# A hand-scheduled RWKV, FP4 FFN and attention kernel: the decay constant goes from VectorE's subtraction to the bias of ScalarE's Relu passes, and every engine's order of calls and waits is rewritten

## Chip, cores, metric

One core of a Trainium2 chip. The metric is device time in microseconds; all data are float32. Engines: PE (TensorE; PEld is its weight load), DVE (VectorE), ACT (ScalarE), POOL (GpSimd), and SP, which issues the transfers.

## What is computed

`x` is 16 sequences of 512 tokens with 128 channels. It passes through an initial layer norm, 4 RWKV layers, an FFN with blockwise FP4 rounding of inputs and weights, a causal attention, and the FFN again, each with a residual. The part that the arithmetic edit touches is the recurrence of an RWKV layer, per channel and over the tokens `t`, with `k`, `v` from the matrix products, `w = exp(time_decay)`, `u = time_first`:

```
a, b, m = 0, 0, -1e38                    # running numerator, denominator, maximum
for t: q = max(m, u + k)                 # the output of the token
       y = (exp(m-q)*a + exp(u+k-q)*v) / (exp(m-q)*b + exp(u+k-q))
       n = max(m - w, k)                 # the state for the next token
       a, b, m = exp(m-w-n)*a + exp(k-n)*v, exp(m-w-n)*b + exp(k-n), n
```

## The kernel before

A job `r` (0 to 63) is one sequence in one RWKV layer: layer `r // 16`, sequence `r % 16`, a tile of 128 partitions by 512. FFN jobs `n` run from 0 to 31 (first FFN, then second), attention jobs from 0 to 15. Each engine has one function with a loop `for t in range(FIRST, TICKS)`, here called ticks. The body of the loop is a list of calls written out by hand, each with a lag: `sub_d(t - 4)` handles job `t - 4` in tick `t`, and does nothing while that job is out of range. So the list and its lags are the engine's order of work; across engines only semaphores tie the ticks together. FFN jobs start at tick 69 (`FFN_AT`), attention at 85, the second FFN at 94, and there the lists mix calls of several parts.

The steps of an RWKV job that the prediction uses, with their lines in the profile:

- DVE: `bn1`, `bn2` (statistics, L230), `variances` (L320, L321), three mixes `mix_rt`, `mix_v`, `mix_t` (L334, L341, L327; from job 10 on; both tensors in SBUF), `scan_pp` (L350, running maximum), `sub_d` (L358), `mul_rv` (L366), `mul_s1` (L373), `scan_bb` (L380), `scan_aa` (L388), `gated` (L396), `rwkv` (L403), `add_xa` (L409), `mix_k`, `mix_r` (L421, L429), `gate` (L436). `init_affine` (L301, L303) runs for the first 16 jobs.
- ACT: `args` (L858, L859: two Relu passes over `dd`, one with scale -1), `seeds` (L882, L884), `exp_r` (L876), `exp_k` (L870), `keep_h1` (L843), `exp_d` (L865), `norm1`, `norm2` (L800), `tanh_r` (L850), `square_1` (L891), `relu` x4 (L912), `square` x2 (L919), `keep_past` (L904), `tanh_c` (L925).
- POOL: `add_xb` (L718), `add_den` (L690), `arg_r` (L684), `norm1_rest` (two chunks of 128, L658), `first_past` (L713, only for the first two jobs of a layer), `rsqrts` (the power, L650, and L652), `mul_y` (L701), `norm2_rest` (three chunks, L658), `sub_dh1` (L677), `scaled_p` (L707), `add_num` (L696).
- PE: `turn1`, `turn2` (L1089), `keys` (L1130), `ff_keys` x4 (L1192), `ff_values` x2 (L1210), `ff_gate` (L1199), `receptance`, `output`, `values` (L1155, L1178, L1143).

The chain through which a job's normalised tile reaches the recurrence is: `norm1_rest` on POOL and `norm1` on ACT, `turn1` on PE (waits for both), `keep_h1` on ACT, and behind it in ACT's order `exp_d`, for which `scan_bb` on DVE waits.

Before: `pp` is the running maximum after the decay; `sub_d` computes `dd = (k + w) - pp`, `args` takes `relu(dd)` and `relu(-dd)`, `arg_r` clips `dd` with `capt = CAP - u + w`, and `exp_r` takes `exp(... + now)` with `now = u - w`. `vecs_done` counts the 7 small vector steps at the start. `Waits.wait_ge` leaves out a wait that an earlier one on the same engine already covers.

Of the kernel before, what the change touches and what calls it, by code (L numbers as in the profile page):

```python
# [8 lines left out]
ALU = mybir.AluOpType  # L9
# [23 lines left out]
LN2_LAG = 6  # L33
# [3 lines left out]
FIRST = -2  # L37
# [39 lines left out]
def hybrid_program(nc, x_in, weights, vecs, rows, fp4w, qkv, wout, mask, ident, out):  # L77
    ctx = ExitStack()
    with ctx:
# [29 lines left out]
        capt, now = sb("capt", [128, L]), sb("now", [128, L])  # L109
# [61 lines left out]
        in_x, capt_done, ready = sem("in_x"), sem("capt"), sem("ready")  # L171
# [41 lines left out]
        VECS = 7  # L213
# [8 lines left out]
        def vector():  # L222
# [74 lines left out]
            def init_affine(b):  # L297
                if 0 <= b < NB:
                    w.wait_ge(small_here, 48)
                    w.wait_ge(n_in.z, b + 1)  # L300
# [9 lines left out]
            def variances(s):  # L310
                if 0 <= s < NR + LN2_LAG:
                    lo, hi = 0 if s < NR else NT, 2 * NT if s >= LN2_LAG else NT
                    rs, st = n_1.rs2[s % 3][:, :, lo:hi], n_1.st2[s % 3][:, lo:hi, :]
                    w.wait_ge(n_1.z, min(s - 2, NR))
# [4 lines left out]
                    w.wait_ge(n_2.stats, s - LN2_LAG + 1)  # L319
# [24 lines left out]
            def scan_pp(r):  # L344
                if 0 <= r < NR:
                    w.wait_ge(vecs_done, VECS)
                    w.wait_ge(consts, PADS)
                    w.wait_ge(d_done, r - 1)
                    w.wait_ge(k_done, r + 1)
# [41 lines left out]
            def gated(r):  # L391
                if 0 <= r < NR:
                    w.wait_ge(rwkv_done, r - 1)
                    w.wait_ge(sr_done, r + 1)
                    w.wait_ge(num_done, r + 1)
# [123 lines left out]
            def a_mask(n, i):  # L519
                if n in range(NB):  # L520
                    last = chunk(pS[i], i)
                    w.wait_ge(att_here, 48)
                    w.wait_ge(sim_mm, NT * n + i + 1)
                    e.tensor_tensor(last, last, msk[:, :], ALU.add).then_inc(msk_done, 1)

            def a_max(n, i):
                if n in range(NB):
                    w.wait_ge(a_x, n - 1)
                    w.wait_ge(msk_done, NT * n + i + 1)
# [8 lines left out]
            def a_add(n):  # L538
                if n in range(NB):
                    w.wait_ge(ari_done, n + 1)  # L540
                    w.wait_ge(a_bias, n + 1)
                    w.wait_ge(pv_mm, n + 1)
# [7 lines left out]
            for t in range(FIRST, TICKS):  # L550
                a_inverse(att_job(t - 5))
                rwkv(t - 6)
                sub_d(t - 4)
                mul_up(ffn_job(t - 4), 0)
                mul_up(ffn_job(t - 4), 1)
                bn2(t - 7)
                fx_sub(ffn_job(t - 2))
                fx_scale(ffn_job(t - 1))
                fh_add(ffn_job(t - 5), 0)
                mix_k(t - 8)  # L560
                mix_r(t - 8)
                mul_up(ffn_job(t - 4), 2)
                gated(t - 5)
                fh_sub(ffn_job(t - 5), 0)
                mul_up(ffn_job(t - 4), 3)
                variances(t - 1)
                fx_inverse(ffn_job(t - 1))
                mix_rt(t - 3)
                mix_v(t - 3)
                fh_max(ffn_job(t - 4))  # L570
                init_affine(t)
                mix_t(t - 3)
                a_mask(att_job(t - 4), 0)
                fh_scale(ffn_job(t - 4))
                a_max(att_job(t - 4), 0)
                fh_add(ffn_job(t - 5), 1)
                fh_inverse(ffn_job(t - 4))
                fh_sub(ffn_job(t - 5), 1)
# [862 lines left out]
```

## Time and profile before

| | us |
|---|---|
| median of 3 runs | 1366.13 |
| lowest, highest | 1358.09, 1373.18 |
| the profiled execution | 1361.77 |
| its span | 1360.5 |

The span runs from the first to the last instruction; 1.3 us lie around it. The granted TensorE clock has a mean of 0.994 of 2.4 GHz. Busy shares of the span: PE 94%, DVE 91%, ACT 90%, POOL 88%.

### The profile page before, as it was taken

The page shows a single profiled execution, that of the slowest core. Times are in us where ns is not written, and L with a number is a line of the kernel's source. Part 1 is how long each engine was busy: PE and PEld are TensorE (multiplying, and loading weights), DVE is VectorE, ACT ScalarE, POOL GpSimd, SP SyncE. Part 2 cuts the span into 40 slices and gives each one's busy share as a digit, 9 for nine tenths or more (in the row PEclk, how much of TensorE's full clock was granted, in tenths as well). Part 3 has the DMA queues.
Part 4 walks back from the last instruction along what each step waited for, and adds up shares of the span by engine and source line. Part 5 has one row for each costly group of instructions (what it writes and reads, how often), then busy time and mean ns, then how long its engine had stood idle before and what let it go on. Part 6 is the DMA issues. An engine that isn't in the chain of part 4 may idle for free.

```text
span 1360.5 us, 23452 instructions
## 1 busy us (share of the span) xinstructions
PE 1272.4 (94%) x7177; PEld 916.7 (67%) x7177; DVE 1243.0 (91%) x2235; ACT 1221.0 (90%) x2347; POOL 1198.7 (88%) x1401
## 2 busy tenths in 40 slices
PE   3789999999999999999999999989999998999997
PEld 1346666766677766767766666766777776678776
DVE  6998999999999999999999999679999477988995
ACT  4789999999999999999999999977787899999875
POOL 6898999999999999999999999989998456765884
PEclk9889999999999999999999999999999999999999
DMA  6020000000000000000000000010000000000011
GB/s 180 0 76 1 1 17 1 1 1 1 1 1 1 2 1 1 1 1 1 1 1 1 1 2 16 25 32 24 16 2 0 1 1 1 1 16 17 25 32 40
DMA packets 26925, 18.55 MB, mean 14 GB/s; under 512 B 1072, under 2 KB 26160, under 8 KB 26800
## 3 DMA queue, kind: packets, MB, share of 16 engines
q1 hardware_dynamic: 26800, 17.05, 4.2%
q8 instruction: 58, 0.95, 0.3%
q14 instruction: 67, 0.55, 0.1%
HBM read 12.85 MB, written 4.19 MB: 13 GB/s over the span
## 4 chain that ended last, share of the span: by engine, by line
PE 42%; POOL 32%; DVE 10%; issue 10%; ACT 5%; DMA 0%; POOLq 0%; SPq 0%; DVEq 0%; ACTq 0%
PE ps L1210 9%; POOL z L658 7%; PE ps L1192 7%; POOL ln_rs L650 4%; PE ps L1089 3%; POOL rv L696 3%; PE ps L1269 3%; PE ps L1319 2%; PE ps L1241 2%; POOL er L690 2%; POOL p L707 2%; PE ps L1248 2%; PE ps L1178 2%; PE ps L1155 2%; POOL W L747 2%
## 5 line engine op out<-in xcount | busy, mean ns | idle before, releaser
L1210 PEld LDWEIGHTS ps<-W,kf 128*128 128x128 f32 x2048 | 243.6, 192 | 31.3 <-issue 31.1
L1210 PE MATMUL ps<-W,kf 128*128 128x128 f32 x2048 | 248.8, 275 | 0.0
L1192 PE MATMUL ps<-xk,W 128*128 128x512 f32 x512 | 241.7, 593 | 0.3
L658 POOL TENSOR_SCALAR z<-X,ln_rs 128x128 f32<-128x128 f32 x320 | 171.6, 550 | 0.3 <-POOL ln_rs L652 0.2
L1192 PEld LDWEIGHTS ps<-xk,W 128*128 128x128 f32 x512 | 91.4, 190 | 90.7 <-issue 70.9
L912 ACT ACTIVATE kf<-ps 128x512 f32<-128x512 f32 x256 | 149.3, 585 | 1.9 <-PE ps L1192 1.9
L1089 PEld LDWEIGHTS ps<-idn,z 128*128 128x128 f32 x664 | 77.9, 142 | 95.4 <-issue 80.2
L1089 PE MATMUL ps<-idn,z 128*128 128x128 f32 x664 | 103.8, 279 | 34.9 <-POOL z L658 27.9
L919 ACT ACTIVATE kf<-kf 128x1024 f32<-128x1024 f32 x128 | 135.2, 1056 | 0.0
L650 POOL TENSOR_TENSOR ln_rs<-ln_rs,mhalf 128x8 f32<-128x8 f32 (+1 forms) x70 | 125.3, 1791 | 5.5 <-DVE ln_rs L321 4.3
L747 POOL TENSOR_TENSOR W<-W,hsc 128x704 f32<-128x704 f32 x64 | 88.8, 1387 | 24.7 <-DVE hsc L499 24.5
L800 ACT ACTIVATE z<-X,ln_rs 128x128 f32<-128x128 f32 x192 | 86.7, 486 | 14.5 <-POOL ln_rs L652 14.5
L1241 PE MATMUL ps<-WG,d 128*128 128x352 f32 x256 | 93.4, 467 | 3.8 <-ACT ed L975 1.3
L1248 PE MATMUL ps<-WU,d 128*128 128x352 f32 x256 | 92.3, 465 | 4.2 <-DVE W L480 4.0
L230 DVE BATCH_NORM_STATS2 ln_st<-X 128x6 f32<-128x256 f32 x256 | 96.2, 415 | 0.0
L904 ACT ACTIVATE past<-ps,vec,cz 128x511 f32<-128x511 f32 x128 | 92.5, 776 | 4.0 <-PE ps L1089 2.5
L753 POOL TENSOR_TENSOR W<-W,hsc 128x704 f32<-128x704 f32 x64 | 88.7, 1386 | 3.1 <-DVE W L511 3.0
L1178 PEld LDWEIGHTS ps<-W,rc 128*128 128x128 f32 x512 | 67.7, 193 | 30.8 <-issue 30.5
L1199 PEld LDWEIGHTS ps<-W,xc 128*128 128x128 f32 x512 | 66.9, 191 | 31.7 <-issue 28.4
L696 POOL TENSOR_TENSOR rv<-rv,aa 128x512 f32<-128x512 f32 x64 | 81.8, 1279 | 6.0 <-DVE aa L388 6.0
L380 DVE TENSOR_TENSOR_SCAN bb<-ps,ed 128x512 f32<-128x512 f32 x64 | 77.8, 1216 | 9.4 <-ACT ps L865 9.0
L718 POOL TENSOR_TENSOR X<-X,cr 128x512 f32<-128x512 f32 x64 | 82.2, 1284 | 2.8 <-DVE cr L436 2.8
(184 smaller groups left out, 3796.2 us busy)
## 6 DMA issues: line engine op xcount, KB each, us to landing
X<-x_in SPq DMA_DIRECT2D x16, 256.0 KB, 4.9
xi<-x_in SPq DMA_DIRECT2D x16, 256.0 KB, 2.8
out<-X SPq DMA_DIRECT2D x16, 256.0 KB, 2.3
W<-weights SPq DMA_DIRECT2D x4, 832.0 KB, 7.1
W<-fp4w SPq DMA_DIRECT2D x1, 560.0 KB, 7.3
row<-rows SPq DMA_DIRECT2D x1, 192.0 KB, 3.0
wqkv<-qkv SPq DMA_DIRECT2D x1, 96.0 KB, 5.5
idn<-ident SPq DMA_DIRECT2D x1, 64.0 KB, 3.3
```

The lines of the kernel that those rows point to most:

```text
L230: last = e.bn_stats(g.of(g.st, n)[:, 2 * k:2 * k + 2, :].rearrange("p a s -> p (a s)"), src[:, k * 256:(k + 1) * 256].rearrange("p (a c) - ...
L650: e.tensor_tensor(rs[:, 0, :], rs[:, 2, :], mhalf[:, 0:hi - lo], ALU.pow).then_inc(*own.next())
L658: last = e.tensor_scalar(chunk(dst, j), chunk(src, j), rs[:, 0, j:j + 1], rs[:, 1, j:j + 1], ALU.mult, ALU.add)
L696: e.tensor_tensor(rv[r % 2][:, :], rv[r % 2][:, :], aa[r % 2][:, 0:T], ALU.add).then_inc(num_done, 1)
L747: e.tensor_tensor(h, h, spread(hsc[n % 2][:, 0, k * 44:(k + 1) * 44], 44), ALU.mult).then_inc(fh_y[k], 1)
L912: e.activation(kf[r % 3][:, f, :], (pF0, pF1)[f % 2][:, :], ACT.Relu).then_inc(relu_done[f], 1)
L919: e.activation(both, both, ACT.Square).then_inc(sq_done[k], 1)
L1089: last = e.transpose(chunk(dst, j), chunk(src, j), idn[:, :])
L1192: e.matmul((pF0, pF1)[f % 2][:, :], w_of(r, WCK + f), xk[r % 2][:, :], start=True, stop=True).then_inc(kf_mm[f], 1)
L1210: last = e.matmul(chunk(pKV, j), kf[r % 3][:, f, j * 128:(j + 1) * 128], w_of(r, WCV + f), start=f == 0 and j == 0, stop=f == 3, skip_grou ...
L1241: e.matmul(pG[j % 2][:, 0:I], chunk(fx[n % 2], j), WG[:, :], start=True, stop=True).then_inc(g_mm, 1)
L1248: e.matmul(pU[j % 2][:, 0:I], chunk(fx[n % 2], j), WU[:, :], start=True, stop=True).then_inc(u_mm, 1)
```

## The change

1. `sub_d` drops the decay: `dd = k - pp` (a plain subtraction of two tensors). `args` adds it back as a bias read per partition: `relu(dd + w)` and `relu(-dd - w)`. `capt` becomes `CAP - u`, `exp_r` takes `u` as its bias, and two small vector steps at the start (and the semaphore between them) go.
2. In each function with several waits the one that the author takes to be met last is written first.
3. The list of calls of each engine gets another order, and the lags are renumbered.

The core of the diff. In the lists, the calls of FFN, attention and set-up jobs are left out where "..." stands, and only the calls for RWKV jobs are shown.

```diff
-FIRST = -2
+FIRST = -21
...
-                e.tensor_scalar(capt[:, :], vec[:, TF, :], -1.0, CAP, ALU.mult, ALU.add).then_inc(capt_done, 1)
+                e.tensor_scalar(capt[:, :], vec[:, TF, :], -1.0, CAP, ALU.mult, ALU.add).then_inc(vecs_done, 1)
...
-                w.wait_ge(capt_done, 1)
-                e.tensor_tensor(capt[:, :], capt[:, :], ew[:, :], ALU.add).then_inc(vecs_done, 1)
-                e.tensor_tensor(now[:, :], vec[:, TF, :], ew[:, :], ALU.subtract).then_inc(vecs_done, 1)
...
             def sub_d(r):
                 if 0 <= r < NR:
+                    w.wait_ge(pp_done, r + 1)
                     w.wait_ge(args_done, r - 1)
                     w.wait_ge(argr_done, r - 1)
-                    w.wait_ge(pp_done, r + 1)
-                    e.scalar_tensor_tensor(out=dd[r % 2][:, :], in0=pK[:, :], scalar=col(ew, r), in1=pp[r % 2][:, 0:T],
-                                           op0=ALU.add, op1=ALU.subtract).then_inc(d_done, 1)
+                    e.tensor_tensor(dd[r % 2][:, :], pK[:, :], pp[r % 2][:, 0:T], ALU.subtract).then_inc(d_done, 1)
...
             def scan_bb(r):
                 if 0 <= r < NR:
+                    w.wait_ge(ed_done, r + 1)
                     w.wait_ge(den_done, r - 1)
                     w.wait_ge(ek_done, r + 1)
-                    w.wait_ge(ed_done, r + 1)
...
-                    e.activation(ed[r % 2][:, 0, :], dd[r % 2][:, :], ACT.Relu)
-                    e.activation(ed[r % 2][:, 1, :], dd[r % 2][:, :], ACT.Relu, scale=-1.0).then_inc(args_done, 1)
+                    e.activation(ed[r % 2][:, 0, :], dd[r % 2][:, :], ACT.Relu, bias=col(ew, r))
+                    e.activation(ed[r % 2][:, 1, :], dd[r % 2][:, :], ACT.Relu, bias=col(wneg, r), scale=-1.0).then_inc(args_done, 1)
...
-                    e.activation(er[r % 2][:, :], er[r % 2][:, :], ACT.Exp, bias=col(now, r)).then_inc(er_done, 1)
+                    e.activation(er[r % 2][:, :], er[r % 2][:, :], ACT.Exp, bias=v_of(r, TF)).then_inc(er_done, 1)
```

The lists of the RWKV calls, lag in brackets, before and after (a later call of the same tick stands further right; `init` calls and those of other parts are left out):

```
DVE  before rwkv(6) sub_d(4) bn2(7) mix_k(8) mix_r(8) gated(5) variances(1) mix_rt(3) mix_v(3) mix_t(3) bn1(0)
            mul_rv(4) mul_s1(4) add_xa(6) scan_bb(4) scan_aa(4) gate(10) scan_pp(3)
DVE  after  rwkv(6) sub_d(4) bn2(7) mix_k(8) mix_r(8) gated(5) variances(1) mix_t(3) mix_rt(3) mix_v(3) add_xa(6)
            mul_rv(4) mul_s1(4) bn1(0) scan_bb(4) scan_aa(4) gate(10) scan_pp(3)
POOL before add_xb(13) add_den(7) arg_r(6) norm1_rest(4) first_past(9) rsqrts(3) mul_y(7) norm2_rest(9)
            sub_dh1(4) scaled_p(7) add_num(6)
POOL after  scaled_p(11) norm1_rest(7) sub_dh1(8) add_xb(16) add_num(10) add_den(10) arg_r(9) first_past(11)
            rsqrts(6) mul_y(10) norm2_rest(12)
ACT  before relu3(11) exp_d(6) norm1(3) tanh_r(6) norm2(9) square_1(7) relu0(10) square0(11) relu1(10) keep_past(9)
            square1(11) tanh_c(10) args(5) seeds(6) exp_r(5) exp_k(5) relu2(10) keep_h1(3)
ACT  after  square0(12) relu1(11) square_1(8) relu0(11) keep_past(10) square1(12) tanh_c(11) relu2(11) args(6)
            seeds(7) exp_r(6) exp_k(6) keep_h1(4) relu3(11) exp_d(6) norm2(9) norm1(3) tanh_r(6)
PE   before turn2(12) ff_keys2(13) ff_keys3(13) ff_values0(14) receptance(8) output(10) values(8) turn1(6)
            ff_values1(14) keys(7) ff_keys0(12) ff_keys1(12) ff_gate(12)
PE   after  turn1(6) ff_values1(14) ff_keys0(12) ff_keys1(12) keys(7) ff_gate(12) turn2(11) ff_keys3(12)
            ff_keys2(12) ff_values0(13) receptance(7) output(9) values(7)
```

Of the other calls, those that move by more than a place: on DVE `fx_max` goes from tick `t` of its job to `t - 1` (one tick later, to the top of the list), `a_mask(3)` and `a_max(3)` from the end of a tick to the top of the next, `a_bn` from `t + 1` to `t - 1`, and `a_add(t - 5)`, the last call but one, to `a_add(t - 6)` just behind `a_inverse(t - 5)`; `fx_add` goes to the next tick too.

## Rows read from the trace of the kernel before

**Rows 1.** The page's part 1: busy time, share of the span, instructions.

```profile
PE 1272.4 (94%) x7177; PEld 916.7 (67%) x7177; DVE 1243.0 (91%) x2235; ACT 1221.0 (90%) x2347; POOL 1198.7 (88%) x1401
```

**Rows 2.** Stretches: length, busy PE, PEld, DVE, ACT, POOL, then clock and DMA.

```profile
561.85:699.62 137.77, 137.10 (x771) 97.67 (x770) 137.77 (x232) 136.88 (x244) 135.34 (x155) 1.00 0.00 1
699.62:845.05 145.43, 137.62 (x767) 96.88 (x766) 140.49 (x226) 135.96 (x239) 143.82 (x155) 1.00 0.01 3
900.00:1050.00 150.00, 140.17 (x793) 104.01 (x792) 147.59 (x259) 115.88 (x243) 141.27 (x156) 0.99 0.05 13
1150.00:1260.00 110.00, 106.98 (x653) 82.82 (x652) 94.70 (x212) 103.37 (x232) 70.43 (x80) 1.00 0.04 11
```

**Rows 3.** Stretches, `sub_d` (L358) alone: length, busy, and in brackets its count.

```profile
174.53:227.93 53.40, 2.94 (x4) 1.00 0.04 11
290.40:383.55 93.15, 5.17 (x7) 1.00 0.00 1
496.15:549.33 53.18, 2.95 (x4) 1.00 0.00 1
561.85:699.62 137.77, 8.06 (x11) 1.00 0.00 1
699.62:845.05 145.43, 8.15 (x11) 1.00 0.01 3
```

**Rows 4.** Timeline of POOL in a short tick: start, length.

```profile
613.94 0.70 POOL L684 TENSOR_SCALAR er<-d,capt 128x512 f32<-128x512 f32 x1
614.61 0.91 POOL L658 TENSOR_SCALAR z<-X,ln_rs 128x128 f32<-128x128 f32 x2
615.63 2.07 POOL L650 TENSOR_TENSOR ln_rs<-ln_rs,mhalf 128x8 f32<-128x8 f32 x1
```

**Rows 5.** Timeline of DVE in the same tick: the first of the three mixes.

```profile
615.45 0.74 DVE L334 SCALAR_TENSOR_TENSOR sr<-dh,vec,h 128x512 f32<-128x512 f32 x1
```

**Rows 6.** Timeline of POOL in a long tick.

```profile
743.67 2.38 POOL L658 TENSOR_SCALAR z<-X,ln_rs 128x128 f32<-128x128 f32 x2
746.02 1.65 POOL L650 TENSOR_TENSOR ln_rs<-ln_rs,mhalf 128x8 f32<-128x8 f32 x1
```

**Rows 7.** Timelines of DVE, PE and ACT in the same long tick.

```profile
743.73 0.79 DVE L334 SCALAR_TENSOR_TENSOR sr<-dh,vec,h 128x512 f32<-128x512 f32 x1
746.20 0.63 PE L1089 MATMUL ps<-idn,z 128*128 128x128 f32 x4 [0.86 <-POOL z L658]
746.95 0.78 ACT L843 ACTIVATE h<-ps,vec 128x512 f32<-128x512 f32 x1 [0.71 <-PE ps L1089]
748.80 1.23 DVE L380 TENSOR_TENSOR_SCAN bb<-ps,ed 128x512 f32<-128x512 f32 x1 [0.45 <-ACT ps L865]
```

**Rows 8.** Timeline of POOL: `first_past` of job 48; `arg_r` beside `init_affine`.

```profile
690.76 0.72 POOL L713 TENSOR_SCALAR past<-cp 128x2 f32<-128x2 f32 x1
...
43.86 1.14 POOL L684 TENSOR_SCALAR er<-d,capt 128x512 f32<-128x512 f32 x1
```

**Rows 9.** Groups, 200 to 900 us: busy, mean ns of one, idle before.

```profile
L358 DVE SCALAR_TENSOR_TENSOR d<-ps,ew,pp 128x512 f32<-128x512 f32 x51 | 37.5, 736 | 0.0
L876 ACT ACTIVATE er<-er,now 128x512 f32<-128x512 f32 x51 | 36.1, 707 | 0.0
L373 DVE TENSOR_TENSOR s<-ed,ps 128x512 f32<-128x512 f32 x51 | 34.4, 674 | 0.0
L870 ACT ACTIVATE ed<-ed 128x512 f32<-128x512 f32 x51 | 31.3, 614 | 0.0
```

**Rows 10.** Timeline of ACT in a short tick: `relu1`, then `keep_past`.

```profile
609.94 0.59 ACT L912 ACTIVATE kf<-ps 128x512 f32<-128x512 f32 x1
610.55 1.45 ACT L904 ACTIVATE past<-ps,vec,cz 128x511 f32<-128x511 f32 x2
```

**Rows 11.** Timelines of ACT and DVE, late: `fx_add`, which has one wait.

```profile
1152.96 0.66 ACT L958 ACTIVATE ps<-z 128x512 f32<-128x512 f32 x1
1153.65 0.69 DVE L465 SCALAR_TENSOR_TENSOR z<-ps,z 128x512 f32<-128x512 f32 x1 [0.53 <-ACT ps L958]
```

More of the change, by code:

```diff
@@ L212, in hybrid_program @@
         W_OPS = 2
-        VECS = 7
+        VECS = 6
         def ffn_job(t):
@@ L550, in vector @@
             for t in range(FIRST, TICKS):
+                a_mask(att_job(t - 5), 3)
+                a_max(att_job(t - 5), 3)
+                fx_max(ffn_job(t - 1))
+                weights_scales(t - 2)
+                a_bn(att_job(t - 1))
                 a_inverse(att_job(t - 5))
+                a_add(att_job(t - 6))
                 rwkv(t - 6)
+                mul_up(ffn_job(t - 4), 0)
                 sub_d(t - 4)
-                mul_up(ffn_job(t - 4), 0)
+                bn2(t - 7)
@@ L578, in vector @@
                 fh_sub(ffn_job(t - 5), 1)
-                init_stats(t + 2)
+                bn1(t)
                 a_mask(att_job(t - 4), 1)
-                prepare(t)
-                bn1(t)
-                mul_rv(t - 4)
-                fx_max(ffn_job(t))
+                scan_bb(t - 4)
                 a_max(att_job(t - 4), 1)
-                mul_s1(t - 4)
-                add_xa(t - 6)
-                weights_scales(t - 1)
-                scan_bb(t - 4)
-                a_mask(att_job(t - 4), 2)
@@ L766, in gpsimd @@
             for t in range(FIRST, TICKS):
-                fh_divided(ffn_job(t - 7), 0)
-                weights_divided(t - 5)
-                fh_scaled(ffn_job(t - 8), 1)
-                f_rsqrt(ffn_job(t - 2))
-                add_bias(att_job(t - 6))
-                add_xb(t - 13)
-                add_den(t - 7)
-                fh_divided(ffn_job(t - 7), 1)
-                add_res(ffn_job(t + 1))
-                arg_r(t - 6)
-                fx_scaled(ffn_job(t - 4))
-                norm1_rest(t - 4)
-                init_rsqrt(t - 1)
-                first_past(t - 9)
-                rsqrts(t - 3)
-                a_rsqrt(att_job(t - 2))
-                fx_divided(ffn_job(t - 3))
-                mul_y(t - 7)
-                weights_scaled(t - 5)
-                fh_scaled(ffn_job(t - 7), 0)
-                norm2_rest(t - 9)
-                sub_dh1(t - 4)
-                scaled_p(t - 7)
-                add_num(t - 6)
+                weights_divided(t - 8)
+                fh_scaled(ffn_job(t - 11), 0)
+                fx_divided(ffn_job(t - 7))
+                add_res(ffn_job(t - 1))
+                scaled_p(t - 11)
+                norm1_rest(t - 7)
+                add_bias(att_job(t - 10))
+                fh_divided(ffn_job(t - 10), 0)
+                sub_dh1(t - 8)
+                add_xb(t - 16)
+                add_num(t - 10)
+                fh_scaled(ffn_job(t - 11), 1)
+                add_den(t - 10)
+                arg_r(t - 9)
+                f_rsqrt(ffn_job(t - 5))
+                fh_divided(ffn_job(t - 10), 1)
+                a_rsqrt(att_job(t - 6))
+                init_rsqrt(t - 4)
+                first_past(t - 11)
+                rsqrts(t - 6)
+                mul_y(t - 10)
+                fx_scaled(ffn_job(t - 7))
+                weights_scaled(t - 8)
+                norm2_rest(t - 12)
         def scalar():
@@ new lines, in scalar @@
+                a_exp(att_job(t - 7), 3)
+                relu(t - 11, 0)
+                keep_hq(ffn_job(t - 9), 2)
+                fx_magic(ffn_job(t - 4))
+                silu(ffn_job(t - 6), 1)
+                keep_past(t - 10)
+                fh_magic(ffn_job(t - 7), 0)
+                keep_fx(ffn_job(t - 5))
+                silu(ffn_job(t - 6), 2)
+                square(t - 12, 1)
+                tanh_c(t - 11)
+                init_z(t - 2)
+                silu(ffn_job(t - 6), 3)
@@ new lines, in scalar @@
+                put_x(ffn_job(t - 9))
+                relu(t - 11, 2)
+                args(t - 6)
+                a_z(att_job(t - 4))
+                keep_hq(ffn_job(t - 8), 0)
+                seeds(t - 7)
+                weights_kept(t - 10, 2)
+                weights_kept(t - 9, 1)
+                fh_magic(ffn_job(t - 7), 1)
+                exp_r(t - 6)
+                keep_hq(ffn_job(t - 8), 1)
+                silu(ffn_job(t - 5), 0)
+                f_z(ffn_job(t - 2))
+                exp_k(t - 6)
```

261 lines of the change are left out of this document (117 added, 144 removed).

## The prediction

> **What bounds the kernel now.** I read the page's busy shares first. Four engines stand at 88 to 94% [rows 1], so no single engine is the answer, and the question is what a tick lasts. The start of `sub_d`, one a tick, gives that. From 561.85 to 699.62 us, 11 ticks take 137.77 us, 12.52 each; from 699.62 to 845.05 the same 11 take 145.43, 13.22 each, with the same work in them [rows 3]. There are two kinds of tick, and three stretches of long ones: 7 + 4 + 11 = 22 ticks in 93.15 + 53.18 + 145.43 = 291.76 us. At 12.52 they would take 275.4, so the long kind costs 16.3 us.
>
> In the short ticks DVE is busy without a gap (137.77 of 137.77), ACT and POOL nearly (136.88, 135.34). In the long ones POOL is the full one (143.82 of 145.43) and DVE waits [rows 2]. POOL's timeline says why. `norm1_rest` takes 0.91 us for two chunks in a short tick and 2.38 in a long one [rows 4, 6]. In the short tick the chunks are over (615.52) just after DVE's mixes start (615.45); in the long one they start at 743.67, with the mixes at 743.73 and beside them all the way [rows 4 to 7]. The power costs 2.07 beside the mixes and 1.65 behind them. So the long tick has 1.47 more on POOL and 0.42 less, 1.05 in all, and what is left of POOL's idle time takes the rest up.
>
> The long tick also keeps itself alive. `norm1_rest` ends late, `turn1` starts at 746.20 after 0.86 idle, `keep_h1` at 746.95 after 0.71, `exp_d` stands behind it, and `scan_bb` starts at 748.80 after 0.45 idle on DVE [rows 7]. DVE is thus set back by POOL and brings its mixes to the same place beside `norm1_rest` again. What throws it there is `first_past`: 0.72 us beside a mix [rows 8], just before job 53's tick, and the other two stretches begin at the same point of their layers.
>
> **The change, part by part.** The sum is made against the profiled execution, 1361.8 us; the median of the three is 4.3 above it, which I take for some five more long ticks of 0.9, and those would go too.
>
> *sub_d.* 736 ns with a scalar read per partition against 674 for a plain two-tensor operation that reads one PSUM operand as it does [rows 9]: 0.06 off DVE each tick, 12.52 to 12.46. *Relu bias.* `exp_r`, whose bias is read per partition, takes 707, `exp_k` with none 614 [rows 9]. Two passes pay 0.093 each, 0.19 a tick on ACT; `exp_r` has such a bias on both sides. ACT's idle time in 11 short ticks is 137.77 - 136.88 = 0.89, 0.08 a tick [rows 2]. One more piece is hidden in its busy time: from `relu1` to `keep_past` the starts are 0.61 apart for an instruction of 0.59 [rows 10], where neighbours that don't wait overlap by about 0.1. So ACT's shortest tick is 12.52 - 0.08 - 0.11 = 12.33, and with the bias 12.52. ACT takes DVE's place as the bound, and a short tick stays as it is: I take +0.02 a tick for 45 ticks, 1 us (bounds: -0.06 if ACT has more hidden slack, +0.11 if the 0.11 isn't there: -3 to +5). In the first ticks, where ACT's chain is waited for, ten ticks pay 0.19: 2 us. The two small steps less at the start are nothing, since `vecs_done` is long there before the first `scan_pp`.
>
> *norm1_rest moved.* In POOL's new list it stands behind `scaled_p`, and `arg_r` is what comes before the power. The power can't start before DVE's `variances`, and the mixes follow that at once, so whatever stands just before the power is what meets the mixes. Laid end to end with the lengths of POOL's timeline (a full tile 1.25 us from start to start, `sub_dh1` 1.0), with `sub_d` at 0 (611.94 in this tick): the power stays at 3.7, `mul_y` at 5.9, `norm2_rest` 7.2, `scaled_p` 8.5, `norm1_rest` 9.7 to 10.6, `sub_dh1` 10.6, `add_xb` 11.6, `add_num` 0.4 of the next tick, `add_den` 1.6, `arg_r` 2.9 to 3.55. `turn1` is at 4.5 of the next tick, so the chain that carried POOL's delay to DVE has 6 us of slack instead of 0.9. That takes away both halves of the long tick: -16.3 us. Four ticks of the run-up (174.53 to 227.93) take 53.40 where 50.1 would do, partly for the same reason; I take half, -1.5 us (0 to -3.3).
>
> *arg_r beside the mixes.* It now runs where `norm1_rest` was. In a short tick it ends at 3.55 with mixes from 3.5, as `norm1_rest` did, and nothing is lost. After `first_past` POOL is 0.6 late for the two jobs, `arg_r` falls beside a mix, and the nearest row has it at 1.14 instead of 0.69 beside two SBUF additions of DVE [rows 8]. It is one instruction where `norm1_rest` is two. The new ties of POOL's lateness: `gated` waits for `add_num` (ends 1.65, wanted 2.6), `seeds` for `add_den` (ends 2.9, wanted 3.0 to 3.9, as ACT runs as late as `scan_bb` allows), `exp_r` for `arg_r`. About 0.9 us of lateness costs nothing. I take 3 us for the six `first_past` (0 to 21, the end below being every tick at +0.48).
>
> On this the Trainium skill speaks against the change ("SBUF — State Buffer", the glossary entry on the shared port pair): DVE and GpSimd share a pair that is taken for a whole instruction, and the other "fully blocks". The rows agree for the short ones: `first_past` needs 0.72, the rest of a mix. By that rule `arg_r` would lose up to a whole mix whenever it starts inside one, and POOL's late tick would not end by itself; that is the second case below.
>
> *Other moves.* `keys` goes behind two `ff_keys` and ends 1.7 later, with `scan_pp` 3 us behind it in the old order: covered. `add_xa` is earlier, `bn1` later, `relu2` before `args`; the 0.5 of `relu2` sits in ACT's slack before `exp_d` (its tensor is ready 0.9 before `scan_bb` in the short tick). `FIRST` only lets `folded` come first, as before; it has no instruction of its own. On SP nothing moves.
>
> *Waits.* `scan_bb`, `keep_h1` and `turn1` wait for several things and write the late one last. `keep_h1` starts 0.12 after the transposes end (746.20 + 0.63), `turn1` 0.15 after POOL ends (746.05) [rows 6, 7]. A call with one wait starts 0.03 after its release (1152.96 + 0.66 to 1153.65) [rows 11]. If the first-written wait is the quick one, each stall that ends on a reordered wait is 0.07 to 0.09 shorter. In the RWKV part these stalls are mostly in the long ticks, which are counted already; for the rest I take 20 stalls, -1.5 us (0 to -4). If the order of writing does the reverse, the loss is of the same size.
>
> *The part from 860 us.* The first FFN has DVE at 147.59 of 150 and its work is unchanged: nothing. Beside the second FFN, attention ticks have PE at 106.98 of 110, DVE at 94.70 [rows 2]; what moves there moves inside DVE's and ACT's slack. `a_inverse` now stands before `a_add` and waits for the last exponential, which in the old order is over a microsecond before `a_add` starts. `fx_max` a tick later takes a wait of DVE out of the change-over. I take -1 us (+6 to -6).
>
> Sum: 1361.8 - 16.3 - 1.5 + 1 + 2 + 3 - 1.5 - 1 = 1347.5; I say 1347.
>
> **The rivals.** *(A) 1347, chance 0.52*, as above.
>
> *(B) arg_r is caught in place of norm1_rest, 1352 to 1370, most likely 1358, chance 0.26.* `add_num`, `add_den`, `arg_r` and the power come in this order, and `gated`, `variances` and the mixes hang on `add_num`. Once POOL is 0.9 late, `arg_r` starts 1.25 behind `add_num` and the mixes 0.9 behind it, so they meet again in each tick. Price: 1.14 - 0.69 = 0.45, a tick of 12.5 + 0.35 to 0.48. For 22 ticks as now 8 to 10 us, for all 45 from the first `first_past` 16 to 22: 1347 - 3 + 8 to 22. For it: the same self-locking was seen, and the power stays contended. Against: POOL has 0.2 a tick to catch up, and one instruction is caught, not two.
>
> *(C) It does nothing, 1360 to 1368, chance 0.13.* ACT's hidden slack isn't there, ticks get 12.6, and the late part gives back 6: 1347 + 5 + 6 and a wait order that costs 1.5 instead of giving it, 1361. The new order would then be worth only what it spends.
>
> *(D) Slower, 1384, chance 0.09.* `arg_r` is held behind two or three mixes, as `norm1_rest` was through its two chunks: the tick is 13.3 again, but without end, since the delay now reaches DVE through `add_num` to `gated` directly and each layer's first jobs renew it. 45 ticks at +0.8 make 36: 1361.8 - 16.3 + 3 + 36 = 1384.5. It decides from a mean tick of 13.2 after job 20. Against it: a mix is 0.74 and `arg_r` is one instruction, and `first_past` was through after one mix.
>
> **How the numbers follow.** About 1% is what a measurement of this kernel can tell from none. Faster by over 1% is below 1352.5: nearly all of A (0.47) and a little of B (0.05), 0.52. Slower by over 1% is above 1379.8: D, 0.09. Between: 0.39. The range: below A the unknown costs reach some 12 us (3 + 3 + 2.5 + 5); above it must take in B and C. 1335 to 1371 leaves out D and the ends, under 2 in 10.
>
> **What would show it.** `norm1_rest`'s two chunks at 0.9 throughout, never 2.4, and `turn1` never waiting for L658. `sub_d` near 674 ns, both Relu passes near 720. The mean tick from job 20 to 63 at 12.5 to 12.6; if it is 12.9, look for L684 above 1.1 (B); 13.3, D. In short ticks ACT is the engine without a gap and DVE waits a little, at `scan_bb`. Reordered waits released after 0.03 to 0.05. The time from job 63's `sub_d` to the end, 515 us now, within 6. The prediction is wrong in its main step if the ticks were long for another reason than the meeting of `norm1_rest` and the mixes, or if POOL's new phase makes `seeds` wait for `add_den` each tick.

## The result and the profile after

The changed kernel takes 1348.84 us (median of 4 runs, 1348.33 to 1349.53) against 1364.45 for the kernel before on the same chip (4 runs, 1358.09 to 1373.18): ratio 0.9883, 95% interval [0.9837, 0.9929]. It is faster by 1.2%, clear of the noise, and it repeats within 1.2 us where the kernel before spreads over 15. The profiled execution took 1348.33 us, with a span of 1347.0 against 1360.5.

The page's busy shares after, to lay beside [rows 1]:

```profile
PE 1274.4 (95%) x7177; PEld 917.2 (68%) x7177; DVE 1241.6 (92%) x2233; ACT 1226.1 (91%) x2347; POOL 1184.8 (88%) x1401
```

POOL lost 13.9 us with the same 1401 instructions; ACT gained 5.1, with the bias in it. Nothing was removed from POOL, so its instructions got shorter. Stretches after, columns as in [rows 2]: nine short ticks, then the three long ones that follow the start of the last layer (jobs 51 to 54):

```profile
568.37:681.24 112.87, 112.17 (x631) 79.96 (x630) 112.87 (x191) 112.58 (x200) 110.63 (x128) 1.00 0.00 1
681.24:721.63 40.39, 39.17 (x211) 26.23 (x210) 39.63 (x64) 38.37 (x68) 39.76 (x44) 1.00 0.01 1
```

And `sub_d` (now L355) alone, as in [rows 3], from job 19 to job 63, then to the end:

```profile
274.16:834.88 560.72, 29.91 (x44) 1.00 0.01 3
834.88:1347.00 512.12, 0.68 (x1) 0.99 0.05 15
```

A short tick is 112.87 / 9 = 12.54 us, and 44 ticks take 560.72 where the kernel before took 845.11 - 277.89 = 567.22. The trains of 7, 4 and 11 long ticks [rows 3] are gone; three per layer are left, longer ones: 40.39 / 3 = 13.46. Groups after, 200 to 900 us, columns as in [rows 9]:

```profile
L654 POOL TENSOR_SCALAR z<-X,ln_rs 128x128 f32<-128x128 f32 x258 | 113.0, 450 | 0.4 <-POOL ln_rs L648 0.4
L680 POOL TENSOR_SCALAR er<-d,capt 128x512 f32<-128x512 f32 x51 | 41.8, 820 | 0.6
L854 ACT ACTIVATE ed<-d,ew 128x512 f32<-128x512 f32 x51 | 37.6, 736 | 0.0
L355 DVE TENSOR_TENSOR d<-ps,pp 128x512 f32<-128x512 f32 x50 | 34.0, 680 | 0.0
L866 ACT ACTIVATE ed<-ed 128x512 f32<-128x512 f32 x51 | 31.3, 614 | 0.0
```

`sub_d` is 680 ns (736 before), a Relu pass 736, a chunk of z on POOL 450. POOL in a short tick after (`sub_d` at 605.99), to lay beside [rows 4]: `arg_r`, the power, and `norm1_rest` in its new place.

```profile
608.86 0.70 POOL L680 TENSOR_SCALAR er<-d,capt 128x512 f32<-128x512 f32 x1
609.73 2.08 POOL L646 TENSOR_TENSOR ln_rs<-ln_rs,mhalf 128x8 f32<-128x8 f32 x1 [0.18 <-DVE ln_rs L318]
...
615.85 0.87 POOL L654 TENSOR_SCALAR z<-X,ln_rs 128x128 f32<-128x128 f32 x2
```

DVE in the same tick, `variances` and the first mix:

```profile
609.17 0.41 DVE L317 TENSOR_SCALAR ln_rs<-ln_st 128x8 f32<-128x8 f32 x1
609.49 0.16 DVE L318 TENSOR_SCALAR ln_rs<-ln_st 128x8 f32<-128x8 f32 x1
609.56 0.74 DVE L324 SCALAR_TENSOR_TENSOR xt<-dh,vec,h 128x512 f32<-128x512 f32 x1
```

`norm1_rest` is 0.87, far from the mixes. But L317, 128x8, takes 0.41 and ends (609.58) when `arg_r` does (609.56): it started 0.31 behind `arg_r` and is held until POOL is through. The first mix starts as `arg_r` ends, and POOL's power waits for L318. So POOL has nearly nothing to spare. POOL behind `first_past`, where the long ticks come from (L686 is `add_den`):

```profile
672.34 0.72 POOL L709 TENSOR_SCALAR past<-cp 128x2 f32<-128x2 f32 x1
...
683.51 1.27 POOL L686 TENSOR_TENSOR er<-er,bb 128x512 f32<-128x512 f32 x1
684.89 1.80 POOL L680 TENSOR_SCALAR er<-d,capt 128x512 f32<-128x512 f32 x1
686.77 0.51 POOL L709 TENSOR_SCALAR past<-cp 128x2 f32<-128x2 f32 x1
...
697.22 1.27 POOL L686 TENSOR_TENSOR er<-er,bb 128x512 f32<-128x512 f32 x1
698.59 1.80 POOL L680 TENSOR_SCALAR er<-d,capt 128x512 f32<-128x512 f32 x1
...
710.78 1.27 POOL L686 TENSOR_TENSOR er<-er,bb 128x512 f32<-128x512 f32 x1
712.03 0.69 POOL L680 TENSOR_SCALAR er<-d,capt 128x512 f32<-128x512 f32 x1
```

DVE in the same three ticks:

```profile
684.41 0.41 DVE L317 TENSOR_SCALAR ln_rs<-ln_st 128x8 f32<-128x8 f32 x1
...
684.81 0.74 DVE L324 SCALAR_TENSOR_TENSOR xt<-dh,vec,h 128x512 f32<-128x512 f32 x1
685.47 0.74 DVE L331 SCALAR_TENSOR_TENSOR sr<-dh,vec,h 128x512 f32<-128x512 f32 x1
686.13 1.10 DVE L338 SCALAR_TENSOR_TENSOR xv<-dh,vec,h 128x512 f32<-128x512 f32 x1
...
697.30 0.69 DVE L392 SCALAR_TENSOR_TENSOR p<-ps,rv 128x512 f32<-128x512 f32 x1 [0.46 <-POOL rv L692]
697.91 0.62 DVE L317 TENSOR_SCALAR ln_rs<-ln_st 128x8 f32<-128x8 f32 x1
...
711.46 0.63 DVE L317 TENSOR_SCALAR ln_rs<-ln_st 128x8 f32<-128x8 f32 x1
712.00 0.74 DVE L318 TENSOR_SCALAR ln_rs<-ln_st 128x8 f32<-128x8 f32 x1
712.65 0.74 DVE L324 SCALAR_TENSOR_TENSOR xt<-dh,vec,h 128x512 f32<-128x512 f32 x1
```

`first_past`, itself beside a mix, has made POOL some 0.7 late. L317 (684.41) therefore comes beside `add_den` and not beside `arg_r`; when `add_den` ends (684.78), L318 and the first mix are in front. `arg_r` starts 0.08 us behind the mix and takes 1.80: two mixes pass, it gets through, and now the third mix is the one that waits (1.10 for 0.74). In the second tick the delay reaches DVE by `gated`, which waits for `add_num` (0.46). In the third tick `arg_r` starts (712.03) before L318 is through and before the mixes (712.65) and takes 0.69; L318 is held instead (0.74 for 0.16), and the next tick is short again. What lets `arg_r` through in the third tick the trace does not say: in the second as in the third, L317 starts about 0.6 before `add_den` ends (697.91 to 698.49, 711.46 to 712.05) and is held until then.

### The profile page after: what moved, and what is told of

It reads as the page before. It is cut to its first block, busy times and chain, and to the rows that moved or that the text cites. A ratio compares the mean times of both kernels' runs of the same rounds, so it can differ in the third digit from the quotient of the medians.

```text
span 1347.0 us, 23396 instructions
## 1 busy us (share of the span) xinstructions
PE 1274.4 (95%) x7177; PEld 917.2 (68%) x7177; DVE 1241.6 (92%) x2233; ACT 1226.1 (91%) x2347; POOL 1184.8 (88%) x1401
## 4 chain that ended last, share of the span: by engine, by line
PE 37%; DVE 24%; POOL 21%; issue 12%; ACT 4%; DVEq 0%; DMA 0%; SPq 0%; POOLq 0%; ACTq 0%
POOL ln_rs L646 5%; PE ps L1205 5%; PE ps L1187 5%; PE ps L1264 4%; DVE aa L384 3%; PE ps L1236 3%; DVE bb L376 3%; POOL z L654 3%; PE ps L1243 3%; PE ps L1314 3%; DVE ln_st L230 2%; PE ps L1084 2%; PE ps L1296 2%; DVE rv L362 2%; PE ps L1252 2%
## 5 line engine op out<-in xcount | busy, mean ns | idle before, releaser
L1187 PE MATMUL ps<-xk,W 128*128 128x512 f32 x512 | 245.2, 598 | 3.3 <-ACT kf L907 3.3
L654 POOL TENSOR_SCALAR z<-X,ln_rs 128x128 f32<-128x128 f32 x320 | 140.7, 451 | 1.0 <-POOL ln_rs L648 0.9
L646 POOL TENSOR_TENSOR ln_rs<-ln_rs,mhalf 128x8 f32<-128x8 f32 (+1 forms) x70 | 129.5, 1850 | 8.9 <-DVE ln_rs L318 8.4
L1187 PEld LDWEIGHTS ps<-xk,W 128*128 128x128 f32 x512 | 86.0, 191 | 70.1 <-ACT kf L907 38.0
L796 ACT ACTIVATE z<-X,ln_rs 128x128 f32<-128x128 f32 x192 | 80.9, 485 | 11.8 <-POOL ln_rs L648 11.8
L697 POOL TENSOR_TENSOR er<-er,rc 128x512 f32<-128x512 f32 x64 | 82.0, 1281 | 0.9 <-ACT rc L879 0.9
```

Of the source, the lines that this page charges most:

```text
L646: e.tensor_tensor(rs[:, 0, :], rs[:, 2, :], mhalf[:, 0:hi - lo], ALU.pow).then_inc(*own.next())
L654: last = e.tensor_scalar(chunk(dst, j), chunk(src, j), rs[:, 0, j:j + 1], rs[:, 1, j:j + 1], ALU.mult, ALU.add)
L1187: e.matmul((pF0, pF1)[f % 2][:, :], w_of(r, WCK + f), xk[r % 2][:, :], start=True, stop=True).then_inc(kf_mm[f], 1)
```

## The experiments

Twelve runs (eleven kernels and the changed one again) were made in four groups, each group on one chip with the kernel before beside it. That kernel's median was 1365.05, 1358.62, 1367.40 and 1368.68 us (1355.6 to 1378.3 over all), so ratios to it move by up to 0.7% from group to group, and I read times as well. The table splits each profiled execution at the starts of `sub_d` of jobs 0, 19 and 63, read from DVE's timeline. One execution of each is split; the two of the changed kernel stand 1.4 us apart in the last part, so differences of about 1 us there tell nothing by themselves.

| kernel | median us | 0 to 19 | 19 to 63 | 63 to the end |
|---|---|---|---|---|
| before | 1364.45 | 245.6 | 567.2 | 515.4 |
| b_arith | 1358.26 | 245.3 | 564.4 | 516.1 |
| b_waits | 1356.65 | 244.8 | 562.7 | 514.9 |
| b_order | 1353.16 | 242.0 | 561.6 | 515.1 |
| a_arith | 1349.76 | 241.7 | 561.4 | 512.0 |
| changed | 1348.84 | 241.5 | 560.7 | 512.1 |
| a_again (changed, once more) | 1349.15 | 241.3 | 560.7 | 513.5 |
| b_norm1 | 1353.69 | 241.0 | 560.9 | 516.5 |
| b_fp | 1361.62 | 248.7 | 567.1 | 516.3 |
| a_n1back | 1377.20 | 248.6 | 582.0 | 512.3 |
| a_fp | 1378.33 | 247.1 | 584.8 | 511.5 |
| a_mixlate | 1363.03 | 247.5 | 565.9 | 513.3 |
| a_fp_dve | 1340.22 | 241.2 | 552.8 | 511.9 |
| b_two | 1343.96 | 240.4 | 551.9 | 517.5 |

### One move alone: b_norm1

```diff
 (before, POOL)
-                norm1_rest(t - 4)
                 init_rsqrt(t - 1)
...
                 scaled_p(t - 7)
+                norm1_rest(t - 3)
```

> The kernel before with one call moved: norm1_rest from before rsqrts to behind scaled_p (lag 3). My theory (norm1_rest beside the mixes makes the long tick, and its tie to scan_bb keeps it): norm1_rest's two chunks stay at 0.9 us, the 22 long ticks of 13.3 go, and arg_r takes them over for a few ticks behind each first_past as in the changed kernel, 8 us lost there: 1350 to 1354, ratio 0.989 to 0.993 against before. Rival (the gain is that of the whole redrawn order, or of the waits): 1360 or more, ratio above 0.996.

1353.69 us (1352.89 to 1354.47), ratio 0.9896 [0.9854, 0.9937]: as my theory had it. The move alone gives 11.4 us of the medians, and the spread is gone with it. Its POOL behind `first_past` shows what the changed kernel shows:

```profile
698.86 1.80 POOL L684 TENSOR_SCALAR er<-d,capt 128x512 f32<-128x512 f32 x1
700.75 0.51 POOL L713 TENSOR_SCALAR past<-cp 128x2 f32<-128x2 f32 x1
...
707.91 0.88 POOL L658 TENSOR_SCALAR z<-X,ln_rs 128x128 f32<-128x128 f32 x2
```

### The move taken back: a_n1back

```diff
 (changed, POOL)
-                norm1_rest(t - 7)
...
                 arg_r(t - 9)
+                norm1_rest(t - 7)
```

> The changed kernel with norm1_rest put back between arg_r and the power (same lag), everything else of the new order kept. My theory: the long ticks are back, norm1_rest at 2.4 us in them, as many as before (about 20 of +0.85): 1358 to 1366, ratio to before 0.995 to 1.002. Rival (the rest of the order or the waits bring the gain): 1350 or less.

1377.20 us (1375.11 to 1379.58), ratio 1.0079 [1.0053, 1.0104], worse than I expected and worse than the kernel before. Of the 51 ticks between jobs 12 and 63 all but two last 12.80 or more, mostly 12.82 and 13.38 in turn. POOL, then DVE, in one of its long ticks:

```profile
616.34 2.40 POOL L654 TENSOR_SCALAR z<-X,ln_rs 128x128 f32<-128x128 f32 x2
```

```profile
616.41 0.79 DVE L324 SCALAR_TENSOR_TENSOR xt<-dh,vec,h 128x512 f32<-128x512 f32 x1
```

This is the meeting of [rows 6, 7]. `arg_r` is caught as well behind each `first_past` (1.80). In the new order the rest of the change is worth nothing without this move.

### first_past, two moves that fail: b_fp and a_fp

```diff
 (b_fp: before, POOL)
-                first_past(t - 9)
...
                 norm2_rest(t - 9)
+                first_past(t - 9)
 (a_fp: changed, POOL)
                 scaled_p(t - 11)
+                first_past(t - 11)
...
-                first_past(t - 11)
```

> The kernel before with one call moved: first_past from just before rsqrts to behind norm2_rest, where no mix runs. It tests the trigger alone: norm1_rest still stands where it is caught. My theory: without the 0.7 us of lateness the ticks stay short to the end, 1361.8 - 16.3 = 1346, ratio 0.985 to 0.990. Rival (long ticks start for another reason, such as the layer's weights or the first jobs of a layer on another engine): long ticks at the same three places, ratio 0.998 to 1.002.

> The changed kernel with one call moved: first_past from between arg_r and rsqrts to behind scaled_p. In the changed kernel arg_r takes 1.80 us beside the mixes in two ticks behind each first_past, and three ticks there last 12.94, 13.71, 13.75 instead of 12.54: 2.8 us three times. My theory: those go, 1348.8 - 8.4 = 1340.5, ratio to before 0.982. Rival (POOL is late by the extra instruction wherever it stands, since it has only 0.15 us of idle a tick): arg_r still meets the mixes, 1347 to 1349.

b_fp: 1361.62 us (1356.81 to 1370.95), ratio 0.9977 [0.9944, 1.001]: no difference that can be told, and not what I expected. `first_past` takes 0.19 in its new place, but the next tick's `arg_r` comes 0.4 later (2.40 behind `sub_d` instead of 2.01), `norm1_rest` takes 2.02, and the train of 13.4 us ticks runs as before. In the run-up jobs 12 to 17 have ticks of 13.1 to 13.4 with no `first_past` near. So `first_past` need not meet a mix to start a train. I take it that any delay of POOL by more than it has to spare does; that is read from these ticks and not tested by itself.

a_fp: 1378.33 us (1377.26 to 1379.80), ratio 1.0085 [1.0056, 1.0114], where I had expected 1340. POOL's timeline:

```profile
691.90 0.19 POOL L709 TENSOR_SCALAR past<-cp 128x2 f32<-128x2 f32 x1 [5.41 <-DVE xc L425]
...
709.77 0.19 POOL L709 TENSOR_SCALAR past<-cp 128x2 f32<-128x2 f32 x1 [4.15 <-DVE xc L425]
```

`first_past` waits for the mixes of the job two before it. So early in POOL's list that wait isn't met: POOL stands 5.41 and 4.15 us and holds `add_num`, which `gated` needs. Two ticks a layer take 17.87 to 19.42. The edit added a wait that I had not looked up.

### The three parts of the change, apart: b_arith, b_waits, b_order, a_arith

```diff
 (b_arith: before with the new arithmetic alone)
-                    e.scalar_tensor_tensor(out=dd[r % 2][:, :], in0=pK[:, :], scalar=col(ew, r), ...
+                    e.tensor_tensor(dd[r % 2][:, :], pK[:, :], pp[r % 2][:, 0:T], ALU.subtract)...
 (b_waits: before with the new order of waits alone, as)
+                    w.wait_ge(ed_done, r + 1)
                     w.wait_ge(den_done, r - 1)
                     w.wait_ge(ek_done, r + 1)
-                    w.wait_ge(ed_done, r + 1)
 (b_order: before with the new lists of calls and FIRST alone)
 (a_arith: b_order and b_waits together, that is the changed kernel with the old arithmetic)
```

> The kernel before, with the arithmetic alone changed: the decay constant leaves the subtraction (a tensor_tensor instead of a scalar_tensor_tensor) and goes into the bias of the two Relu passes; order of calls and of waits as before. My theory: this part is worth nothing, as in the prediction's sum: the subtraction loses 0.06 us (0.74 to 0.68), the two Relu passes gain about 0.1 us each (0.63 to 0.73), and neither engine's sum sets the long ticks, which are GpSimd meeting VectorE's mixes; ratio to the kernel before 0.999 to 1.004, 1363 to 1370 us. Rival: the arithmetic is what shortened the kernel, since VectorE is the busiest engine; then 63 jobs by 0.06 us are 3.8 us and the ratio is about 0.997. Second rival: ScalarE becomes the bound by 0.2 us in each of 63 jobs, 1377 us, ratio 1.009.

> The kernel before, with the order of the waits inside each function alone changed (the wait that is met last is written first); arithmetic and order of calls as before. My theory, from the traces of before and after: where the last wait is written first, an instruction starts 0.03 us (VectorE, ScalarE), 0.08 us (GpSimd) or 0.05 us (TensorE) after its releaser instead of 0.10, 0.15 and 0.14; in the stretches with one job after another few instructions wait, so the loops there lose almost nothing, but the run-up, the part after the last job and the long ticks are chains of waits: 1 to 6 us off, ratio 0.996 to 0.999. Rival: the order of waits carries most of the gain (15 us, ratio 0.989), because the recurring loops pass some ten such waits in each tick. A second rival: no effect at all, ratio within 0.001 of 1.

> The kernel before, with the lists of calls of all engines taken from the changed kernel and the first tick at minus 21 as there; arithmetic and order of waits as before. My theory: nearly all of the gain is here, since norm1_rest leaves the place in front of the power on GpSimd: ratio 0.988 to 0.992, 1348 to 1354 us, with ticks of about 12.5 us and three long ones behind each layer's second first_past. Rival: the gain needs the other two parts as well, because GpSimd has only about 0.1 us to spare before the mixes and the later releases use it up: then the long ticks stay through most of a layer and the ratio is 0.996 to 1.002.

> The changed kernel with the old arithmetic (the subtraction adds the decay constant, the Relu passes have no bias), its order of calls and waits kept. My theory: within 2 us of the changed kernel, ratio to the kernel before 0.987 to 0.990: VectorE's subtraction takes 0.06 us more, so its tick is 12.58 to 12.60 instead of 12.54 in the stretches without long ticks (up to 63 x 0.06 = 3.8 us more, against which the mixes start 0.06 us later and GpSimd's arg_r has so much more room ahead of them). Rival: ScalarE bound the changed kernel, and without the biases its tick shortens by up to 0.2 us, 1340 us, ratio 0.982.

- b_arith: 1358.26 (1354.88 to 1364.67), 0.9984 [0.9954, 1.0014]. Nothing.
- b_waits: 1356.65 (1354.62 to 1364.21), 1.0001 [0.9982, 1.0019]. Nothing that can be told; of the 1 to 6 us that I expected, the interval leaves up to some 2.5.
- b_order: 1353.16 (1352.85 to 1353.42), 0.9955 [0.9939, 0.9971]. The time that I expected; the gain in ratio is smaller, as the kernel before was at 1358.62 on this chip.
- a_arith: 1349.76 (1349.21 to 1350.21), 0.9929 [0.9913, 0.9946].

So order gives 5.5 us of the medians of this group, the waits 3.4 on top of it (1353.16 to 1349.76), the arithmetic 0.6 to 0.9 more (against 1349.15 and 1348.84, both of other groups). The 5.5 is small because the kernel before was fast on this chip: b_order's time is that of b_norm1, 1353.16 and 1353.69, so the rest of the new lists adds next to nothing to the one move. By the table the waits' gain is in the part after the last job, 515.1 to 512.0. Without the new order they gave only 0.5 there.

Nine short ticks of a_arith, to lay beside the nine of the changed kernel above:

```profile
569.46:682.50 113.04, 112.18 (x631) 79.90 (x630) 113.04 (x191) 112.74 (x199) 110.81 (x128) 1.00 0.00 1
```

A tick is 12.56 here and 12.54 with the bias, and ACT's idle time is 0.03 a tick in both, so that its busy time tells nothing. What does tell: without the bias ACT has 0.2 us less to do (two passes at 0.64 instead of 0.74), and the tick is no shorter. DVE's `sub_d` costs 0.06 more here, but DVE did not step in as the bound: L320 (L317 in the changed kernel) is held here too, 0.35 for 0.16. So neither of the two sets this tick. The pair of before and b_arith says the same in the old order: in jobs 41 to 49 the ticks are 12.53 and 12.52.

### The cure: a_again, a_fp_dve, a_mixlate

```diff
 (a_fp_dve: changed; first_past leaves POOL, same waits and operation on DVE)
                 variances(t - 1)
+                first_past(t - 7)
                 mix_t(t - 3)
 (a_mixlate: changed, DVE)
+                add_xa(t - 6)
                 mix_t(t - 3)
...
-                add_xa(t - 6)
                 mul_rv(t - 4)
```

> The changed kernel itself, once more, on the chip on which the next two run, since the time of the kernel before has stood 6 us apart between two chips. Every theory: 1348 to 1350 us, with little spread, as in its first four runs and as the changed kernel with the old arithmetic (1349.8).

> The changed kernel with first_past on VectorE, one tick after its wait is met and right ahead of the three mixes, instead of on GpSimd between arg_r and the power. My theory: the 8 us that each kernel still loses in three long ticks of each layer come from first_past making GpSimd's tick longer than the 0.1 us it has to spare, so that the next arg_r (1.80 us instead of 0.69) falls beside the mixes. Without it on GpSimd, and with VectorE's mixes 0.1 us later in just those ticks, no arg_r is caught: ticks of 12.54 to 12.65 through the layers, 1339 to 1342 us, ratio to the changed kernel 0.994. Rival: the long ticks behind each layer's start do not come from first_past but from what the layer's first jobs bring otherwise (the pads of the zeroed parities, the weights): 1348 to 1350 us, unchanged. A second rival, as the two earlier moves of first_past had it: it costs more on the new engine, since a VectorE instruction ahead of the mixes delays a chain from the mixes to the scans: 1350 to 1360 us.

> The changed kernel with add_xa moved from behind the three mixes to in front of them on VectorE, so that the mixes start 0.6 us later in every tick; first_past stays where it was. My theory: arg_r on GpSimd now has about 0.7 us ahead of the mixes instead of 0.1, so that first_past's 0.2 to 0.7 us no longer pushes the next arg_r into them: no ticks of 13.7 us, 1339 to 1343 us; the power starts 0.2 us after arg_r's end and still meets the mixes, 1.65 to 2.1 us as before. Rival: the room in front of the mixes is not what counts; the meeting merely moves on to the two chunks of norm2_rest or to the keys that wait for the first mix, the scan of the maximum (pp) comes 0.6 us late, and all ticks grow: 1350 to 1385 us.

a_again: 1349.15 us (1348.09 to 1350.32), ratio 0.987 [0.983, 0.9909]. a_fp_dve: 1340.22 us (1339.64 to 1341.39), ratio 0.9805 [0.9766, 0.9844], and 1340.22 / 1349.15 = 0.993 of the changed kernel (0.992 to 0.995 by the ends of both sets of runs). DVE, then POOL, at the same jobs as above:

```profile
679.87 0.15 DVE L416 TENSOR_SCALAR past<-cp 128x2 f32<-128x2 f32 x1
679.94 0.74 DVE L324 SCALAR_TENSOR_TENSOR xt<-dh,vec,h 128x512 f32<-128x512 f32 x1
```

```profile
679.17 0.69 POOL L687 TENSOR_SCALAR er<-d,capt 128x512 f32<-128x512 f32 x1
...
691.78 0.69 POOL L687 TENSOR_SCALAR er<-d,capt 128x512 f32<-128x512 f32 x1
```

`arg_r` is 0.69 in both jobs and the two ticks are 12.61. From job 19 to 63 it takes 552.79, 7.9 less than the changed kernel: nearly all of the 8.3 that the nine long ticks there cost.

a_mixlate: 1363.03 us (1360.01 to 1365.71), ratio 0.9966 [0.9937, 0.9994], and the rival's case. My theory is right that no `arg_r` is caught: it takes 0.68 on average, and there are no ticks of 13.7. But nearly every tick is 12.79, and two are 14.4 (jobs 14 and 22, where the other kernels have one of 13.0). POOL in one of them:

```profile
592.66 1.65 POOL L646 TENSOR_TENSOR ln_rs<-ln_rs,mhalf 128x8 f32<-128x8 f32 x1 [0.18 <-DVE ln_rs L318]
594.38 0.36 POOL L648 TENSOR_TENSOR ln_rs<-ln_rs 128x8 f32<-128x8 f32 x1
594.71 1.77 POOL L697 TENSOR_TENSOR er<-er,rc 128x512 f32<-128x512 f32 x1
```

The power no longer meets the mixes (1.65 for 2.08), but what follows it does: +0.16 on the product, +0.50 on `mul_y`. 12.54 - 0.43 + 0.16 + 0.50 = 12.77. The place just behind the power was dearer than the power's own.

### Two moves alone: b_two

```diff
 (before, POOL; first_past is defined on DVE, as in a_fp_dve)
-                norm1_rest(t - 4)
-                first_past(t - 9)
...
                 scaled_p(t - 7)
+                norm1_rest(t - 3)
 (before, DVE)
                 variances(t - 1)
+                first_past(t - 7)
```

> The kernel before with two small moves and nothing else of the change: norm1_rest behind scaled_p, as in the run that took 1353.7, and first_past on VectorE ahead of the mixes, as in the run that took 1340.2. My theory: the gain of the redrawn order lies in norm1_rest's place, and what is left behind each layer's start in first_past's; the spans' excess over ticks of 12.57 (8.7 us in the run with norm1_rest alone) goes, 1344 to 1347 us, with little spread. Rival: first_past on VectorE is only free in the new order, since in the old one the delay of the mixes meets something else; 1350 to 1356 us. Against the run of 1340.2 it should still be 4 to 6 us longer, by the part after the last job, where order and waits together gave 3 to 4.

1343.96 us (1343.24 to 1344.69), ratio 0.9829 [0.9749, 0.9909]. The kernel before with two calls moved is 5 us faster than the whole change, and the 44 ticks are as short as they get (551.9). Against a_fp_dve it is 3.7 longer: 5.6 in the last part (517.5 against 511.9), where the new order and the new waits together count, less 1.7 in the two others. a_fp_dve is the fastest kernel of the study.

## Why the prediction was right, and where it was not

The total was 1347.5, measured 1348.33 in the profiled execution and 1348.84 in the median, and case A with it. By stages it is less good: misses of +5.8 us (job 19 to 63) and -4.5 us (the run-up) cancel, so that the total came within 1.3 us is luck; the main step is not.

- **norm1_rest moved, -16.3: right.** The pair is 0.87 to 0.88 throughout, the trains are gone, and b_norm1 (this move alone) and a_n1back (all but this move) show that it carries the change. The prediction's guess that the runs' median lay above the profiled one by more long ticks fits too: the kernels without this meeting repeat within 2.6 us (a_mixlate, with a meeting of its own, 5.7), those with it spread over 4 to 20.
- **arg_r beside the mixes, +3: mis-sized.** It is the term that failed most. From job 19 to 63 the sum had -16.3 + 1 + 3 = -12.3, measured 560.7 - 567.2 = -6.5. It was priced from `arg_r` at 1.14 beside two additions [rows 8]; beside the mixes it measured 1.80, in two ticks behind the start of the second, third and fourth layer, with a third long tick behind them. The nine ticks stand 8.3 above 12.54 (121.2 for 112.9), inside the bounds of 0 to 21; the whole stretch stands 8.9 above 44 ticks of 12.54 (560.72 - 551.8). a_fp_dve took the long ticks away and got 7.9 back. Case B's mechanism is thus real, for two ticks at a time. By the rule of the Trainium skill ("SBUF — State Buffer", the shared port pair) the prediction reckoned that a caught `arg_r` loses up to a whole mix and that the late tick does not end by itself. That each side is held by the other's instruction the trace does show: 1.80 for 0.69 on POOL, 1.10 for 0.74 and 0.74 for 0.16 on DVE. But `arg_r` lost 1.11, more than a mix of 0.74, and the lateness ends in the third tick. Why it ends is open. It is not that `gated` holds DVE back: in b_norm1 `gated` starts 2.63 to 2.65 behind `sub_d` in all three ticks, as always, and the third `arg_r` is free (0.69) all the same.
- **"About 0.9 us of lateness costs nothing": wrong.** It counted only the waits of `gated` and `seeds`, and not where `arg_r` stands against DVE's small steps and mixes. In a short tick `arg_r` starts 0.31 ahead of L317; 0.7 of lateness turned the two round and cost 8.3 us. In the old order 0.4 was enough to start a train (b_fp), and without the lateness (a_fp_dve) the long ticks are gone.
- **The short tick, 12.54: right number, wrong engine, before and after.** The prediction took DVE for the bound before, since it is busy without a gap, and ACT after. But part of DVE's busy time before is spent held: in the short tick of [rows 4] L320 and L321 last until `norm1_rest` ends (615.52).

```profile
615.18 0.18 DVE L320 TENSOR_SCALAR ln_rs<-ln_st 128x8 f32<-128x8 f32 x1
615.27 0.27 DVE L321 TENSOR_SCALAR ln_rs<-ln_st 128x8 f32<-128x8 f32 x1
```

  The two take 0.31 where nothing holds them and 0.48 a tick here (jobs 41 to 49), so DVE had 0.17 to spare, and the 0.06 that `sub_d` saves goes into it: 0.53 in b_arith, with the tick unchanged. In the changed kernel they take 0.55, 0.51 in a_arith. The short tick is then POOL's: its instructions, the 0.18 in which it waits for L318, which stands behind the held L317, and 0.08 behind the power. That POOL sets it is read from the traces; no run shortened POOL alone.
- **The run-up, -1.5 + 2: mis-sized.** Measured -4.0 (245.56 to 241.54). b_norm1 alone gives -4.6, so the meeting cost more there than the 3.3 us of excess that the prediction saw, and not half of them; and the bias, for which I took 2, costs nothing there (241.7 in a_arith).
- **Waits, -1.5 (0 to -4): right in kind, small in size.** Measured -3.4 on top of the new order. Releases shorten about as forecast. In b_waits `scan_bb` starts 0.03 behind `exp_d` (0.10 before) and `keep_h1` 0.04 behind `turn1` (0.12 before), medians of 13 to 20 stalls; `turn1` starts 0.10 behind POOL (0.15 before), one stall. `scan_bb` behind `exp_d` in the run-up after the change, ACT and DVE:

```profile
93.88 0.59 ACT L861 ACTIVATE ps<-ed 128x512 f32<-128x512 f32 x1
```

```profile
94.51 1.23 DVE L376 TENSOR_TENSOR_SCAN bb<-ps,ed 128x512 f32<-128x512 f32 x1 [0.20 <-ACT ps L861]
```

  93.88 + 0.59 to 94.51 is 0.04. Why the same waits gave 0.5 in the old order's last part and 3.1 in the new one's is open.
- **The part from 860 us, -1: right in size.** Order alone gave -0.3 there, less than two executions of one kernel differ by.
- **Two slips.** The costs under the range add up to 13.5, not 12. The first long tick of the last layer is job 52's, not 53's. Nothing else rests on either.

## What to carry to other kernels

When two engines take turns with the same memory, look in the trace for an instruction whose time has two values, lay the other engine's timeline beside it, and move the shorter or the less urgent of the two by a few microseconds, once for each such pair. Then ask what stands in the vacated place, and what stands behind it: the meeting moves on, and its price is that of the new neighbour. What counted here was how late an engine can be before the two meet, not its idle time in all: two instructions of 0.2 us in sixteen ticks cost 2.8 us. An instruction's busy time can also be time in which it is held, so an engine without a gap need not be the bound. And before you move a call, look up which wait it takes along.

## What the runs showed of the hardware

- A POOL instruction on 128x512 started 0.08 us behind the first of three DVE instructions on SBUF alone was through only after two of them (1.80 for 0.69), in the changed kernel and in b_norm1, b_order, a_arith and a_n1back; started 0.6 us ahead of them it took 0.69.
- It goes both ways and for tiny instructions: a DVE operation on 128x8 took 0.16 alone, and 0.41, 0.62 and 0.74 beside POOL's 128x512.
- Beside the same three mixes the price was 0.43 for the power (2.08 for 1.65), 0.50 for a 128x512 product (1.77 for 1.27), 1.11 for `arg_r`, 1.5 for two chunks of 128x128 (2.40 for 0.87).
- A bias read per partition made a Relu pass over 128x512 0.74 us long (0.64 without), and a stall that ends on the wait written first was 0.07 us shorter on DVE and 0.08 on ACT.
- The kernel before had medians of 1358.6 to 1368.7 us in five groups of runs, the changed kernel 1348.8 and 1349.2 in two: the kernels in which `norm1_rest` can meet the mixes vary from run to run, the others hardly. That this comes of the meeting fits every run; what sets it off in one run and not in another is open.
